# AdaLN attention block with two feed-forward nets: first query and key products together by feature halves, GpSimd and Vector work reordered, last stage reordered

## What is computed

```python
# x: 8 sequences of 128 tokens, 256 features; cond: 8 x 256; H = 16 heads of 128
ada = cond @ ada_w + ada_b             # shift1, scale1, gate1, shift2, scale2, gate2
x1 = ln(x) * (1 + scale1) + shift1
q, k, v = split(x1 @ qkv_w + qkv_b)
a = softmax(q k^T / sqrt(128)) v       # per head and sequence
x = x + gate1 * (a @ out_w + out_b)
x2 = ln(x) * (1 + scale2) + shift2
x = x + gate2 * (gelu(x2 @ ffn_w1 + b1) @ ffn_w2 + b2)
h = square(relu(x @ tern(W_fc).T))     # tern: weights in -s, 0, s by groups of 64
return x_in + rms_norm(h) @ tern(W_proj).T
```

## Time and profile before

| | |
|---|---|
| median of 3 runs | 348.85 us (348.67 to 349.53) |
| profiled execution | 349.12 us, its span 347.3 us |
| TensorE busy | 340.4 us, 98% |
| VectorE busy | 222.2 us, 64% |
| ScalarE busy | 220.7 us, 64% |
| GpSimd busy | 148.4 us, 43% |

### The profile page before, as it was taken

One profiled execution on the slowest core, in us unless ns is written; L12 is line 12 of the kernel. 1 busy time (PEld: TensorE's weight loads), 2 busy tenths in 40 slices (PEclk: granted clock), 3 DMA queues, 4 the chain that ended last, 5 costly groups with the idle time before them and its releaser, 6 DMA issues.

```text
span 347.3 us, 5880 instructions
## 1 busy us (share of the span) xinstructions
PE 340.4 (98%) x1950; PEld 293.5 (85%) x1950; DVE 222.2 (64%) x386; ACT 220.7 (64%) x560; POOL 148.4 (43%) x140
## 2 busy tenths in 40 slices
PE   8999999999999999999999999999999999999985
PEld 7888888889888888888888888888887888889875
DVE  6676756554555664456466454585785888579776
ACT  2773466567566657756664675667589636877583
POOL 3661339736534964644595573488341100000000
PEclk9999999999999999999999999999999999999998
DMA  6953003200300320030030002010000000000002
GB/s 177 364 193 121 3 0 121 63 0 3 121 0 0 121 60 0 0 121 0 15 105 0 0 6 115 2 60 0 4 0 2 0 2 0 0 2 1 1 32 91
DMA packets 12338, 16.53 MB, mean 48 GB/s; under 512 B 720, under 2 KB 8992, under 8 KB 12320
## 3 DMA queue, kind: packets, MB, share of 16 engines
q1 hardware_dynamic: 12136, 16.16, 14.1%
q10 hardware_dynamic: 184, 0.15, 0.1%
HBM read 15.25 MB, written 1.05 MB: 47 GB/s over the span
## 4 chain that ended last, share of the span: by engine, by line
PE 71%; issue 20%; DVE 4%; ACT 4%; POOL 1%; POOLq 0%; ACTq 0%
PE bank L1235 16%; PE bank L1237 15%; PE bank L1236 15%; PE bank L1322 8%; PE bank L1305 7%; PE bank L1311 4%; PE bank L1434 2%; PE bank L1449 1%; ACT prob L579 1%; DVE hid_lo L893 1%; DVE yT L968 1%; ACT hbuf L718 1%; DVE o_lo L952 1%; ACT o_hi L532 1%; ACT hid_hi L493 1%
## 5 line engine op out<-in xcount | busy, mean ns | idle before, releaser
L391 POOL TENSOR_TENSOR prob<-prob,rinv 128x512 f32<-128x512 f32 x32 | 36.3, 1134 | 60.6 <-DVE rinv L1026 60.3
L579 ACT ACTIVATE prob<-bank,negmax 128x128 f32<-128x128 f32 x128 | 45.4, 365 | 25.7 <-DVE negmax L1013 25.6
L1322 PEld LDWEIGHTS bank<-probT,vals 128*128 128x128 f32 x256 | 33.3, 191 | 3.2 <-issue 0.8
L952 DVE SCALAR_TENSOR_TENSOR o_lo<-bank,bias,o_hi 128x512 fp32r<-128x512 f32 x32 | 23.8, 745 | 17.3 <-ACT o_hi L532 17.3
L532 ACT ACTIVATE o_hi<-bank,bias 128x512 fp32r<-128x512 f32 x32 | 21.9, 685 | 19.6 <-PE bank L1322 19.6
L1322 PE MATMUL bank<-probT,vals 128*128 128x128 f32 x256 | 33.9, 275 | 0.0
L350 POOL TENSOR_TENSOR wqk_lo<-raw_qk,wqk_hi 128x512 fp32r<-128x512 f32 x16 | 20.7, 1294 | 19.7 <-ACT wqk_hi L493 18.2
L488 POOL TENSOR_TENSOR xr<-raw_qk,xt 128x256 f32<-128x256 f32 x1 | 0.7, 722 | 66.1 <-ACT raw_qk L796 66.1
L1013 DVE TENSOR_REDUCE negmax<-bank 128x4 f32<-128x512 f32 x32 | 21.8, 681 | 7.8 <-PE bank L1305 7.8
L1235 PE MATMUL bank<-wv_hi,x_hi 128*128 128x512 f32 x62 | 26.1, 420 | 0.0
L579 ACT ACTIVATION_READ_ACCUMULATOR prob<-bank,negmax 128x1 f32 x128 | 26.0, 203 | 0.0
(11 more groups left out here) (218 smaller groups left out, 972.2 us busy)
## 6 DMA issues: line engine op xcount, KB each, us to landing
raw_qk<-in_L_cond_qkv_w_dram SPq DMA_DIRECT2D x6, 512.0 KB, 4.5
raw_v<-in_L_cond_qkv_w_dram SPq DMA_DIRECT2D x4, 512.0 KB, 4.0
raw_o<-in_L_cond_out_w_dram SPq DMA_DIRECT2D x4, 512.0 KB, 3.6
t_w<-in_L_cond_ada_w_dram SPq DMA_DIRECT2D x1, 1024.0 KB, 8.5
raw_w<-in_L_cond_ffn_w_dram SPq DMA_DIRECT2D x2, 512.0 KB, 6.8
t_raw<-in_L_ffn_W_fc_dram SPq DMA_DIRECT2D x4, 256.0 KB, 3.8
t_raw<-in_L_ffn_W_proj_dram SPq DMA_DIRECT2D x4, 256.0 KB, 4.0
raw_qk<-in_L_cond_ffn_w_dram SPq DMA_DIRECT2D x1, 1024.0 KB, 4.8
```

The costliest lines, as they stand in the source:

```text
L391: nc.gpsimd.tensor_tensor(e, e, rinv[:, j % 2, :].unsqueeze(2).broadcast_to([P, SQ, P]), ALU.mult).then_inc(norm_done, 1)
L579: e = nc.scalar.activation(prob[:, j % 2, s, :], bank[BS][:, s * P:(s + 1) * P], ACT.Exp, bias=negmax[:, j % 2, s:s + 1], accum_out=rowsum ...
L952: nc.vector.scalar_tensor_tensor(out=lo[:, :], in0=bank[BO][:, :], scalar=bias[:, bass.ds(HG * G + VB + j % HG, 1)], in1=hi[:, :].bitcast( ...
L1322: m = nc.tensor.matmul(bank[BO][:, s * P:(s + 1) * P], vals[:, b, h], probT[:, s, :], start=True, stop=True)
```

## The change

1. Query and key of head 0 are computed together (`first_qk`), feature half 1 first. `modulate_first` splits the work by sequences: Vector takes sequences 0 and 1, ScalarE 2 and 3, each for half 1 and then half 0. The transposes (L1463 before) run half 1 first. The three identity products after `transpose_raw` are gone.
2. `scores(0, 0)` stands between the two last matmuls of the first values; quad 1's transposes come after the values of sequences 1 and 2; `scores(0, 1)` and the first softmax transpose stand ahead of the modulation products.
3. Four bias loads move from SyncE's to ScalarE's queue, ahead of its table load. Half of the copy of transposed raw x, and the lo part of weight slice 1, move to Vector. GpSimd normalises unit (0,0) ahead of its weight work.
4. In the pair units the first matmul of product 5 stands ahead of product 7 (`pair_p5_begun`). Value block 6 goes to bank BQ and 7 to BE, and waits are split so that product 1 needs block 6 alone.
5. In the last group GpSimd makes w1_lo later, two of its slices only after Vector's `gated`; ScalarE makes `o_hi` ahead of w2_hi in unit 6, and the last `o_hi` after the first gelu.
6. In the ternary stage `finish(0)` and `finish(1)` stand together at c = 3, `finish(2)` and `finish(3)` at c = 5. ScalarE does relu later than the hi part at c = 0 and, at the last chunk, the square ahead of the hi part.

```diff
-        V_AT = {3: ((4, BQ), (5, BK), (6, BE), (7, BQ)), 5: ((0, BQ), (1, BK)), 6: ((2, BQ),), 7: ((3, BK),)}
+        V_AT = {3: ((4, BQ), (5, BK), (6, BQ), (7, BE)), 5: ((0, BQ), (1, BK)), 6: ((2, BQ),), 7: ((3, BK),)}
+        W1_LO_AT = {2: (0,), 4: (1,), 5: (2, 3)}
...
@@ GpSimd
-                    for n in W1_AT.get(j, ()):
+                    if j == 5:
+                        pool.wait_ge(gated, KD)
+                    for n in W1_LO_AT.get(j, ()):
                         w1_lo_part(n)
...
-            wqk_lo_part(1, 2)
             rstd_of(1)
             pool.wait_ge(xn_done, 2)
+            unit(0, 0)
             wqk_lo_part(2, 3)
             pool.wait_ge(wqk_in, 32)
             weight_sums(0, 3, 4, 0)
-            for j in range(2):
-                unit(0, j)
+            wqk_lo_part(3, 4)
+            unit(0, 1)
...
@@ ScalarE
+            def modulate_first():
+                act.wait_ge(ada_ready, 1)
+                for k, src, full, hi in ((1, bank[7], m1_a, hi1_a), (0, bank[6], mod_a, xs_hi)):
+                    act.wait_ge(xt0_done, KD - k)
+                    for b in range(SQ // 2, SQ):
+                        m = nc.scalar.activation(xq0[:, k, b * P:(b + 1) * P], src[:, b * P:(b + 1) * P], ACT.Identity,
...
+                    act.wait_ge(full, 1)
+                    hi_part(x_hi[:, k, SQ // 2 * P:SQ * P], xq0[:, k, SQ // 2 * P:SQ * P], hi)
...
@@ Vector
-            modulate(0, SHIFT1, SCALE1, bank[0:2])
+            modulate_first()
+            dve.wait_ge(xraw_mm, 1)
+            nc.vector.tensor_copy(xT[:, 1, cols(0)], bank[BS][:, :]).then_inc(xT1_done, 1)
             dve.wait_ge(small_cp, 4)
             keep_q0(0, 0, 1)
+            dve.wait_ge(wqk_h, 2)
+            nc.vector.tensor_tensor(wqk_lo[:, :, P:2 * P], raw_qk[:, :, P:2 * P], wqk_hi[:, :, P:2 * P].bitcast(F32),
+                                    ALU.subtract).then_inc(wqk_l, 1)
...
-                if c in (3, 4):
-                    finish(c - 3)
+                if c == 3:
+                    finish(0)
+                    finish(1)
+                if c == 5:
+                    finish(2)
+                    finish(3)
...
@@ TensorE, pair_unit
                 pv(*before(G, j, 1))
+                if j == 4:
+                    pe.wait_ge(v_done, v_count(G, 7))
+                pair_p5_begun(g, a)
                 pair_p7(g, a)
-                pair_p5(g, a)
+                pair_p5_ended(g, a)
                 out_half(*before(G, j, 2), 0)
...
@@ TensorE, prologue
             transpose_raw(0, (bank[BE], bank[BS]))
-            keep_awake(3)
...
+            first_qk()
             first_values()
-            pe.wait_ge(small_cp, 4)
-            pe.wait_ge(xT_done, 1)
-            scores(0, 0)
             qk_products(1, 0, 0)
+            v_block(0, 1, V_FIRST[1])
+            pe.wait_ge(xT_done, 1)
+            v_block(0, 2, V_FIRST[2])
             transpose_x(1, bank[6:8])
-            v_block(0, 1, V_FIRST[1])
-            v_block(0, 2, V_FIRST[2])
+            scores(0, 1)
+            transpose_p(0, 0)
```

More of the change, by code:

```diff
@@ L641, in unit @@
                     keep_k1(HG - 1, NG - 1, 8)
+                o_hi_part(*before(G, j))
+                if last and j == 6:
                     w2_hi_part(2)
-                o_hi_part(*before(G, j))
                 if not last:
@@ L686, in _ @@
             wqk_hi_part(3, 32)
+            keep_v(1, 2, V_FIRST[1])
+            keep_v(2, 3, V_FIRST[2])
             modulate(1, SHIFT1, SCALE1, bank[6:8])
-            for b in range(1, SQ):
-                keep_v(b, b + 1, V_FIRST[b])
+            keep_v(3, 4, V_FIRST[3])
             act.wait_ge(max_done, 2)
@@ L1427, in transpose_raw @@
                         pe.wait_ge(x0_in[s // 2], 16)
-                    for k in range(KD):
-                        m = nc.tensor.transpose(dst[k][:, s * P:(s + 1) * P], xt[:, quad * SQ + s, k * P:(k + 1) * P], ident[:, :])
+                    m = nc.tensor.transpose(dst[:, s * P:(s + 1) * P], xt[:, quad * SQ + s, k * P:(k + 1) * P], ident[:, :])
+                return m
+            def transpose_raw(quad, dst):
+                for k in range(KD):
+                    m = transpose_raw_half(quad, k, dst[k])
                 m.then_inc(xraw_mm, 1)
@@ L1479, in _, with first_qk @@
             transpose_raw(0, (bank[BE], bank[BS]))
[L1480 to L1482 removed]
+            def first_qk():
+                dsts = (bank[BQ], bank[BK])
                 pe.wait_ge(wqk_h, 1)
[L1485 to L1488 removed]
                 for k in (1, 0):
[L1490 to L1494 removed]
+                    if k:
+                        pe.wait_ge(hi1_d, 1)
+                        pe.wait_ge(hi1_a, 1)
+                    else:
+                        pe.wait_ge(hi0_d, 1)
+                        pe.wait_ge(xs_hi, 1)
+                    for w in (wqk_hi, wqk_lo):
+                        if w is wqk_lo:
+                            pe.wait_ge(wqk_l, 1)
+                        for n in range(2):
+                            nc.tensor.matmul(dsts[n][:, :], w[:, n * KD + k, 0:P], x_hi[:, k, cols(0)],
+                                             start=k == 1 and w is wqk_hi, stop=False)
+                pe.wait_ge(bias_in, 64)
+                nc.tensor.transpose(bank[4][:, 0:NBIAS - NA], brow, ident[0:NBIAS - NA, 0:NBIAS - NA]).then_inc(small_t, 1)
+                for k in (1, 0):
+                    pe.wait_ge(xs_lo, KD - k)
+                    for n, done in ((0, q_mm), (1, k_mm)):
+                        m = nc.tensor.matmul(dsts[n][:, :], wqk_hi[:, n * KD + k, 0:P], x_lo[:, k, cols(0)], start=False, stop=k == 0)
+                        if k == 0:
+                            m.then_inc(done, 1)
             def first_values():
@@ L1524, in _ @@
             ada_product(GATE1 + 2, GATE1 + 4, ada_w2, bank[7])
-            scores(0, 1)
-            transpose_p(0, 0)
             pe.wait_ge(xs_lo, 2 * KD)
```

155 lines of the change are left out of this document (80 added, 75 removed).

## The result

The changed kernel takes **346.71 us**, median of 5 runs (346.24 to 347.15), against 348.85 before: ratio 0.9933, 95% interval 0.9918 to 0.9948. The forecast was 346.65 with a range of 345.3 to 348.1, so the size is right. Whether the steps are right is another question, and several of them were not. (346.71 and 348.85 are medians and differ by 2.14; the ratio is one of means, 0.67% or 2.34 us.)

A forecast was written before the change was run, and what follows sets the result against it. TensorE bounds the kernel, busy 340.4 of 347.3 us, so only late starts can gain. Prologue 0.15, loop 0.3, last group 0.6, gelu 0.2 and ternary 0.95 sum to 2.2: 348.85 - 2.2 = 346.65 us, range 345.3 to 348.1.

The forecast's parts named there:

- loop: Unit 4: product 1's wait of 0.1 goes in three groups, 0.3 gained; product 5 ahead of product 7 counted 0.
- last group and first gelu: Last group: late starts from GpSimd's division and Vector's o_lo go, 0.6; the late start at the first gelu goes, 0.2.
- ternary: Ternary stage: idle 1.29 us at an output row goes, 1.55 gained; new wait for lo part 6 costs 0.6; net 0.95.
- First query to scores: Prologue: first query starts near 11.0 and scores of head 0 at 15.4 instead of 16.42, a gain of 0.8.
- Vector takes the lo part of slice 1: Prologue: the row takes up to 1.25, done at 16.3 against a need at 16.6, and costs TensorE nothing.
- Quad 1's modulation: Prologue: TensorE waits from 24.25 to about 24.8 for the scaling of quad 1, a new wait of 0.5.
- x_lo of quad 1: Prologue: Vector's two rows end near 27.8 against a need at 27.7, a new wait of 0.15.
- ScalarE's four DMA issues: Prologue: they hold ScalarE at most 0.46 us each, 1.8 in all; counted 0, bound a loss of 0.2.
- No new waits: Rival: ScalarE or Vector quicker than laid out, so the waits of 0.5, 0.15 and 0.6 stay away; 345.4 us, chance 0.18.
- Vector as the bound: Rival: extra Vector rows in prologue and ternary stage cut the gain to 1.1; 347.75 us, chance 0.16.
- The clock: Rival: TensorE falls to its slower clock near 11 us without the identity products, losing 2.7; 349.35 us, chance 0.03.
- The pair units waiting for u3: Rival: product 4 starts late behind product 7 in 12 pair units, 0.2 each; 348.9 us, chance 0.03.

The follow-up runs named there:

- run 6: Changed kernel with quad 1's transposes and modulation each moved one value block ahead; 346.64 us, ratio 0.9929.
- run 8: Version with three edits, with the four loads of bias rows back on SyncE's queue; 345.76 us, ratio 0.9898.
- runs of part 1 and 4: Kernel before with each of four parts alone (prologue 349.43, loop 348.23, last group and gelu 348.39, ternary 347.97 us); with only ScalarE's last-group orders, 348.66 us.
- three edits: Changed kernel with quad 1's transposes and modulation sooner, output rows of sequences 2 and 3 later, square root of quad 0 before a square; 345.99 us.
- experiment 5: Changed kernel with the output rows of sequences 2 and 3 moved behind the lo part of chunk 7; 346.45 us, ratio 0.9927.

## Why the prediction was right, and where its steps were not

The mechanism is right for the most part: starts that came late come in time, two of the three new waits were foreseen, and the four parts, run alone, gain or lose in their own stretches. That the time is right to 0.06 us is luck to a good part: the loop gave three times its forecast, the prologue nothing.

| term | forecast gain | measured: in the changed kernel's trace; alone in a trace; alone by the runs |
|---|---|---|
| prologue (Q - T) | 0.15 | -0.10; -0.10; -0.5 |
| loop (L - Q) | 0.3 | 0.94; 0.97; 0.80 |
| last group and first gelu (M - L) | 0.8 | 0.74; 0.71; 0.73 |
| ternary (E - M) | 0.95 | 0.87; 0.88; 0.98 |
| sum | 2.2 | 2.46; 2.46; 2.0 |

The changed kernel by its own runs: 2.34 by the ratio, 2.14 by the medians.

- *First query to scores, "1.0 less 0.2 is a gain of 0.8".* Mis-sized: 0.48. From T to the scores it is 0.71 less, and a product of 0.23 now stands behind them. From the first query to the first lo value product it took 4.40 us (11.15 to 15.55) where I had counted 4.2; the first query itself was 0.15 later than laid out, 0.08 of it by the later start.
- *"Vector takes the lo part of slice 1", up to 1.25.* It took 0.82, and cost TensorE nothing.
- *Quad 1's modulation, 0.5.* Right: 0.43 idle and 0.10 of slower products behind it, and run 6 got 0.56 back. With the 0.48 above that is the prologue's loss. The sign "1.8 or more" between the transposes' end and the modulation products read 1.7 (25.04, where the transposes' eight starts from 22.41 end near 23.3). *x_lo of quad 1, 0.15:* did not come.
- *ScalarE's four DMA issues, 0.* Right for what it named: the copy of the condition was at 4.40 after 4.37. What it did not name is the queue they left, which then issued the later loads sooner (run 8).
- *Loop.* The step that failed most. "I take 0.1 us of that as the wait, the rest as the usual start": it was 0.19 a group. "I count 0" for product 5: it was 0.4 in all, beyond the bound of 0.2. What was called "no more than a trace" is 0.10 in each of twelve units, less what u3 takes back.
- *Last group, 0.6, and gelu, 0.2.* Right in the sum, and by the mechanism named: GpSimd's division, o_hi, and Vector's chain, which takes back what is gained ahead of it (runs of part 1 and 4). Mis-sized in the split: 0.4 and 0.3. The gelu's wait has a slower product behind it (0.34 at 263.62 to 263.96 where 0.23 is the pace), which was not counted.
- *Ternary, 1.55 less 0.6.* Right in both halves: the new wait costs 0.55 and 0.10 of slower products behind it. The lateness at the sums of squares, 0.34, comes after the forecast wait and was not named; before it was 0.3 as well.
- *Rivals.* No new waits: two of the three came. Vector as the bound: it holds for two places only, the lo part of chunk 6 and the sums of squares. The clock: from 9 us on no run shows a row of transposes 0.21 apart, and the row for 11 to 12 us, with the gap ahead of the first query, has the clock at 1.00 (windows of the changed kernel: busy time and instructions of TensorE, granted clock, DMA share, GB/s):

```profile
10.00:11.00 1.00, 0.96 (x9) 1.00 0.91 287
11.00:12.00 1.00, 0.85 (x4) 1.00 1.03 366
```

The Trainium skill (TensorE: Matmul & The Clock Gate, Part 4: PE-mode transpose) spoke for that rival; 16 transposes (9.02 to 10.8 us) and a gap of 0.3 did not bring the clock down here. The pair units waiting for u3: seen, at 0.07 a unit where 0.2 was feared, and paid for by u2.

## What to carry to other kernels

When a product is moved ahead, look at what stood between a producer and its consumer there: here the early transposes were left where they were, and TensorE came to the modulation before ScalarE had done it. Output rows that nobody waits for belong in the idle time of the engine that makes them, and the pause ahead of a reciprocal at the end held two exactly. Before a wait is removed, look at the next one: what was gained at the root was waited away within 11 us, because Vector's rows there came no sooner. And compare parts of a trace between two marks of the same engine that enclose the change closely, not by absolute times: at the end that told 0.02 us apart, where up to twelve runs of a version left 0.4 open.

## What the runs showed of the hardware that I had not expected

**The start scatters by half of what the change is worth.** The identity products at the start keep a spacing of 0.21 us, and then the spacing goes over to 0.11, in three profiles only in the modulation products behind them. I read the two as TensorE's slower and faster level (1.2 and 2.4 GHz), since one is twice the other. Over 14 profiles the last wide spacing began between 5.39 and 7.81 us, and T lay between 8.31 and 9.52. The second run of these products in two of them, the one with the last group's part alone and the one with three edits:

```profile
4.38 2.39 PE L1439 MATMUL bank<-ident 128*128 128x128 f32 x14
```
```profile
4.38 3.35 PE L1485 MATMUL bank<-ident 128*128 128x128 f32 x14
```

The granted clock stands at 1.00 in all of it, so this column does not bear the reading out; only the spacing does. The runs of the kernel before lie within 1.4 us of each other (348.38 to 349.77 in the largest set), as T does within 1.2; that the one comes from the other fits, but T is known of the profiled runs alone. No version changed anything ahead of it but the place of the bias loads, and what sets the moment was not tried.

**Vector's cast stood still while GpSimd worked.** In the run of experiment 5 the weights were late (8.95), and so was GpSimd's lo part of them. Vector's timeline, then GpSimd's, then TensorE's:

```profile
9.20 0.73 DVE L897 TENSOR_SCALAR xq<-bank,ada 128x128 f32<-128x128 f32 x2 [0.30 <-PE bank L1514]
9.96 1.11 DVE L901 CAST x_hi<-xq 128x256 fp32r<-128x256 f32 x1
```
```profile
9.66 1.27 POOL L350 TENSOR_TENSOR wqk_lo<-raw_qk,wqk_hi 128x512 fp32r<-128x512 f32 x1 [2.87 <-ACT wqk_hi L493]
```
```profile
11.18 0.70 PE L1546 MATMUL bank<-x_hi,wqk_hi 128*128 128x512 f32 x2 [0.78 <-DVE x_hi L901]
```

The cast of 256 columns took 1.11 us instead of the 0.29 it takes in the five other profiles of this prologue. It ended at 11.07, just behind GpSimd's row (9.66 + 1.27 = 10.93), and TensorE waited 0.78. Against T the first query came 0.60 later than in the changed kernel, and 0.38 of that is left at Q (19.60 against 19.22). GpSimd's row was not longer for it. The scalings that read PSUM take 0.41 and 0.40 beside the same GpSimd row in the changed kernel. The Trainium skill (SBUF — State Buffer, Who interferes with whom) has the rule: casts between SBUF tensors can take a pair of ports that Vector shares with GpSimd, and whoever comes second is blocked to the end. The trace agrees, 10.93 against 11.07. In the changed kernel GpSimd's row ends at 10.17 and the cast starts at 10.52, so by these two numbers a load some 0.35 us later is enough, an estimate that fits the one case seen. The halved prologue has that narrow place, the prologue of before, whose cast started at 11.09, has more room.
